# Edge masks in four 32-row products, output terms of the delta scan on VectorE, 18 chunks beside attention

## The reference

```python
# attn_a: 32 heads of 8, window 128, blocks of 128 tokens
dist = bs + r - c
valid = (dist >= 0) & (dist <= window) & (key_global >= 0)
scores = jnp.where(valid[None, None], scores, finfo.min)
out = softmax(scores) @ vw ; out @ Wo.T
# ffn: 4-bit weights plus rank-16 LoRA, 256 -> 1024 -> 256, relu
# attn_b: rms, q/k/v = silu(silu(causal_conv4(h @ W.T))), q and k l2-normed, beta = sigmoid(h @ Wbeta.T)
def step(S, inp):                      # one token, per head S is 8 x 8
    kt, qt, vt, bt = inp
    err = jnp.einsum('bhvk,bhk->bhv', S, kt) - vt
    S = S - bt[..., None, None] * err[..., None] * kt[..., None, :]
    o = jnp.einsum('bhvk,bhk->bhv', S, qt)
    return (S, o)
# then rms(o) @ Wout.T added, rms, x + (silu(gate) * up) @ Wdown.T
```

## Time and profile before

| | |
|---|---|
| median of 3 runs | 1243.53 us |
| the profiled execution | 1244.26 us, span 1242.3 us |
| busy: TensorE, VectorE, ScalarE, GpSimd | 1037.7, 917.8, 495.8, 179.0 us |
| mean granted TensorE clock | 0.905 |
| a full body (one period, ffn product L1503 of block 4 to that of block 5) | 662.1 to 797.2 us |

### The profile page before, as it was taken

The page is one execution under the profiler, slowest core; times in us unless marked ns, Lnnn a source line. Parts: engine busy times, 40 slices in busy tenths (PEclk is TensorE's granted clock), DMA queues, the critical chain, the costliest instruction groups (busy, mean ns, idle before and its releaser), DMA issues.

```text
span 1242.3 us, 23054 instructions
## 1 busy us (share of the span) xinstructions
PE 1037.7 (84%) x9098; PEld 712.3 (57%) x9112; DVE 917.8 (74%) x2425; ACT 495.8 (40%) x1027; POOL 179.0 (14%) x267
## 2 busy tenths in 40 slices
PE   3589869967998999899988999899989978966467
PEld 2245635645556665666566755666566646744445
DVE  2733277898789778987898778977898678968911
ACT  2034254326443554326432644355443634541122
POOL 2200001040004000400040000300040004010400
PEclk9579879886999899989999999989998979997768
DMA  9813014302430133012410242014400200020000
GB/s 285 153 35 76 17 43 102 61 1 72 101 50 1 35 109 79 9 35 81 89 28 10 77 100 45 1 42 103 82 7 26 82 16 1 18 77 0 5 21 9
DMA packets 94123, 67.81 MB, mean 55 GB/s; under 512 B 47744, under 2 KB 86848, under 8 KB 94016
## 3 DMA queue, kind: packets, MB, share of 16 engines
q1 hardware_dynamic: 88544, 60.75, 20.9%
q10 hardware_dynamic: 4960, 5.54, 1.6%
q0 software_dynamic: 512, 0.05, 0.1%
HBM read 45.57 MB, written 20.32 MB: 53 GB/s over the span
## 4 chain that ended last, share of the span: by engine, by line
PE 47%; DVE 28%; ACT 9%; DMA 7%; SPq 4%; issue 3%; POOL 1%; ACTq 0%; DVEq 0%; POOLq 0%
PE bank L1612 6%; PE bank L1503 5%; PE bank L1757 5%; PE bank L1560 4%; PE bank L1684 4%; PE bank L1766 4%; PE bank L1592 4%; DMA q_l<-lane_q 4%; PE bank L1709 3%; DVE state L1235 3%; DVE lane_buf L1213 3%; PE bank L1555 3%; DVE state L1227 3%; DVE u_l L1222 2%; DVE mx L1023 2%
## 5 line engine op out<-in xcount | busy, mean ns | idle before, releaser
L715 ACT ACTIVATE probs<-bank 128x512 f32<-128x512 f32 x256 | 152.1, 597 | 187.4 <-PE bank L1597 187.3
L1612 PE MATMUL bank<-probs,v_ext 128*9 128x128 f32 x2048 | 164.9, 283 | 16.5 <-ACT probs L715 6.8
L1023 DVE TENSOR_REDUCE mx<-bank 128x2 f32<-128x320 f32 x256 | 120.9, 486 | 54.3 <-PE bank L1560 50.3
L341 POOL TENSOR_TENSOR lane_buf<-state,q_l 128x128 f32<-128x128 f32 x128 | 79.9, 654 | 339.7 <-DVEq L1242 339.7
L1757 PE MATMUL bank<-feat_c,wgu 128*128 128x256 f32 (+1 forms) x384 | 96.3, 402 | 23.6 <-DVE hid_c L1284 18.0
L1612 PEld LDWEIGHTS bank<-probs,v_ext 128*9 128x9 f32 x2048 | 91.3, 93 | 39.6 <-issue 18.0
L1592 PE MATMUL bank<-q_stack,k_stack 128*128 128x128 bf16 x1024 | 106.0, 229 | 2.7 <-DMA q_stack<-m_rows 2.7
L1555 PE MATMUL bank<-edge_mask,identb 128*128 128x128 bf16 x256 | 63.0, 246 | 52.6 <-DVE mx L1023 36.6
L1757 PEld LDWEIGHTS bank<-feat_c,wgu 128*128 128x128 f32 (+1 forms) x384 | 71.8, 192 | 44.1 <-DVE hid_c L1284 21.2
L1213 DVE TENSOR_TENSOR lane_buf<-state,til 128x128 f32<-128x128 f32 x256 | 84.5, 330 | 16.9 <-POOL lane_buf L602 10.2
L1560 PE MATMUL bank<-k_stack,q_stack 128*32 128x160 bf16 x2048 | 93.0, 265 | 0.0
(11 more groups left out here) (169 smaller groups left out, 1762.5 us busy)
## 6 DMA issues: line engine op xcount, KB each, us to landing
k_pieces<-conv SPq DMA_DIRECT2D x48, 128.0 KB, 2.3
k_stack<-k_pieces SPq DMA_DIRECT2D x32, 192.0 KB
k_stack<-k_pieces SPq DMA_DIRECT2D x32, 128.0 KB
k_l<-lane_k SPq DMA_DIRECT2D x8, 512.0 KB, 3.7
q_l<-lane_q SPq DMA_DIRECT2D x8, 512.0 KB, 5.7
q_pieces<-conv SPq DMA_DIRECT2D x24, 128.0 KB, 2.1
q_stack<-q_pieces SPq DMA_DIRECT2D x32, 96.0 KB
tok<-in_x SPq DMA_DIRECT2D x8, 256.0 KB, 3.2
```

Source lines behind the costliest of these rows:

```text
L715: act.activation(probs[:, u % 2], score_bank[u % 2][:], ACT.Exp, scale=float(DK) ** -0.5).then_inc(exp_done, 1)
L1023: dve.tensor_reduce(mx[:, g, 2 * v:2 * v + 2], bank[1 + u % 2][:].rearrange("p (h k) -> p h k", h=2)[:, :, 0:SPAN], AX.X, ALU.max).then_in ...
L1612: last = pe.matmul(bank[5][row:row + VE, col:col + W], v_ext[:, b, kb, h, :], probs[:, u % 2, (hp * 2 + kb) * W:(hp * 2 + kb + 1) * W], st ...
```

## The change

1. **Edge masks.** The one full product (128 columns of the identity, output to 128 rows) becomes four, each with 32 columns of the identity and output to 32 rows.
2. **Output terms.** GpSimd's terms go. For each half VectorE now does one `step_terms` (128 x 1024 outputs) and one `state_terms` (128 x 2048). `mm_` is stored by chunk, and the terms by chunk, so that the innermost runs are 4 and 8 neighbours. For that ScalarE copies the queries into `q_t` in four parts (`queries_out`, 128 x 256 each, in attention steps 14 to 17, over `sqk`) and the states of each half into `s_t` (`states_out`, 128 x 512, over `til`). `scanned` now fires twice, after chunk 21 and after chunk 31.
3. **Order.** Slots: 3 or 4 in steps 18 to 24, 2 in steps 25 to 32, which makes 18 chunks beside the attention. `CUTS` = 18, 21, 22 and `LATE_CUTS` = 22, 24, 26, 29, 32. `first_sums` and the first half's terms come before `act_of(s, 4)`.

```diff
@@ -57,6 +57,7 @@
 TURN_AT = 20
+QUERIES_AT = 14, 15, 16, 17
 UPG = HPH // 2
@@ -162,7 +163,7 @@
         v_l = sqk[:, 1].rearrange("p (v t) -> p v t", v=VR)
-        mm_ = sb("mm_", [128, C, C, NC_])
+        mm_ = sb("mm_", [128, NC_, C, C])
         til = sb("til", [128, NC_, C, KV])
@@ -172,7 +173,10 @@
-        out_terms = lane_buf[:, 0:VR * W // 2 * (DK + C)].rearrange("p (v c i e) -> p v c i e", v=VR, i=C, e=DK + C)
+        out_terms = lane_buf[:, 0:VR * W // 2 * (DK + C)].rearrange("p (c v i e) -> p c v i e", v=VR, i=C, e=DK + C)
+        q_t = sqk[:].rearrange("p s x -> p (s x)").rearrange("p (c i k) -> p c i k", i=C, k=DK)
+        s_t = til[:].rearrange("p c i k -> p (c i k)").rearrange("p (a x) -> p a x", a=2)[
+            :, :, 0:NC_ // 2 * VR * DK].rearrange("p a (c v k) -> p a c v k", v=VR, k=DK)
         o_l = k_l[:].rearrange("p k t -> p (k t)")[:, 0:VR * W].rearrange("p (v c i) -> p v c i", v=VR, i=C)
...
@@ -332,20 +337,21 @@
-        def terms_of(engine, cs, steps=range(C)):
-            qc = q_l[:].rearrange("p k (c i) -> p i c k", i=C)
-            n_c = cs.stop - cs.start
-            for i in steps:
-                for v in range(VR):
-                    engine.tensor_tensor(out_terms[:, v, :, i, 0:DK].rearrange("p c (k e) -> p c k e", e=2),
-                                         state[:, cs, v, :, C:C + 2],
-                                         qc[:, i, cs, :].rearrange("p c (k e) -> p c k e", e=2), ALU.mult)
-                last = engine.tensor_tensor(
-                    out_terms[:, :, :, i, DK:DK + C],
-                    mm_[:, i, :, cs].rearrange("p j (o c) -> p o c j", o=1).broadcast_to([128, VR, n_c, C]),
-                    u_l[:, cs].rearrange("p c v j -> p v c j"), ALU.mult)
-            return last
+        def step_terms(engine, half):
+            cs = slice(half * NC_ // 2, (half + 1) * NC_ // 2)
+            return engine.tensor_tensor(
+                out_terms[:, :, :, :, DK:DK + C],
+                mm_[:, cs].rearrange("p c (o i) j -> p c o i j", o=1).broadcast_to([128, NC_ // 2, VR, C, C]),
+                u_l[:, cs].rearrange("p c v (o j) -> p c v o j", o=1).broadcast_to([128, NC_ // 2, VR, C, C]), ALU.mult)
+        def state_terms(engine, half):
+            cs = slice(half * NC_ // 2, (half + 1) * NC_ // 2)
+            return engine.tensor_tensor(
+                out_terms[:, :, :, :, 0:DK],
+                s_t[:, half].rearrange("p c v (o k) -> p c v o k", o=1).broadcast_to([128, NC_ // 2, VR, C, DK]),
+                q_t[:, cs].rearrange("p c (o i) k -> p c o i k", o=1).broadcast_to([128, NC_ // 2, VR, C, DK]), ALU.mult)
@@ -559,11 +565,6 @@
-            def first_terms(n):
-                pool.wait_ge(scanned, n + 1)
-                terms_of(pool, slice(0, NC_ // 2)).then_inc(terms_ready, 1)
             def ffn_bias(n):
@@ -589,7 +590,7 @@
                 for i in range(C):
-                    last = pool.tensor_copy(mm_[:, i, 0:i + 1, :], pair_l[:, at:at + i + 1, :])
+                    last = pool.tensor_copy(mm_[:, :, i, 0:i + 1].rearrange("p c j -> p j c"), pair_l[:, at:at + i + 1, :])
                     at += i + 1
...
@@ -721,6 +721,23 @@
                 act.copy(o_rows, bank[5][:]).then_inc(o_copied, 1)
+            def queries_out(n, part, front):
+                if part == 0:
+                    act.wait_ge(til_ready, n + 1)
+                    if front:
+                        act.wait_ge(turned_next, n + 3)
+                cs = slice(part * NC_ // 4, (part + 1) * NC_ // 4)
+                act.copy(q_t[:, cs].rearrange("p c i k -> p k (c i)"),
+                         q_l[:].rearrange("p k (c i) -> p k c i", i=C)[:, :, cs].rearrange("p k c i -> p k (c i)")
+                         ).then_inc(q_turned, 1)
+            def states_out(n, half):
+                act.wait_ge(scanned, n * 2 + half + 1)
+                act.copy(s_t[:, half].rearrange("p c v (k e) -> p (c v k) e", e=2),
+                         state[:, half * NC_ // 2:(half + 1) * NC_ // 2, :, :, C:C + 2].rearrange("p c v k e -> p (c v k) e")
+                         ).then_inc(s_copied, 1)
@@ -742,6 +759,8 @@
                                 piece_third(n + 1, s)
+                    if u in QUERIES_AT and after_p:
+                        queries_out(n - 1, QUERIES_AT.index(u), front)
                     if u == TURN_AT:
@@ -855,18 +874,25 @@
                 if following:
+                    if scan:
+                        states_out(t, 0)
                     norm_a(n, 1)
                 if tail:
                     nc.scalar.preload_act_table_set(SILU_SET)
                     gate_of(s, 0)
                     gate_of(s, 1)
                     gate_of(s, 2)
+                if scan and not following:
+                    for part in range(4):
+                        queries_out(t, part, False)
                 if following:
                     turn_a(n, 2)
                 for pair in range(FT // 2):
                     if following:
                         relu_a(n, 2 * pair)
                         relu_a(n, 2 * pair + 1)
+                    if following and scan and pair == IT - 4:
+                        states_out(t, 1)
                     if tail and pair < IT - 3:
...
@@ -956,9 +989,9 @@
         for step in range(BEGIN, N_UNITS + 1):
-            n_slots = 4
+            n_slots = 3 + step % 2 if step >= 18 else 4
             if step in PASS1:
-                n_slots = 3 - step % 2 if PASS1[step][0] else 2
+                n_slots = 2
             SLOT_AT.append(SLOT_AT[-1] + n_slots)
@@ -966,8 +999,8 @@
         OUT_AT = {SLOT_AT[step - BEGIN] + 1: g for g, step in enumerate((11, 19, 27))}
-        CUTS = SLOT_AT[-1] // 4, 23, 24
-        LATE_CUTS = 24, 26, 28, 30, NC_
+        CUTS = SLOT_AT[-1] // 4, 21, 22
+        LATE_CUTS = 22, 24, 26, 29, NC_
@@ -1240,22 +1273,26 @@
                         dve.nop().then_inc(scanned, 1)
+                    if c == NC_ - 1:
+                        dve.nop().then_inc(scanned, 1)
                 return other
             def reduce_terms(half):
                 cs = slice(half * NC_ // 2, (half + 1) * NC_ // 2)
-                return dve.tensor_reduce(o_l[:, :, cs], out_terms, AX.X, ALU.add)
-            def first_sums(n):
-                dve.wait_ge(terms_ready, n + 1)
-                dve.wait_ge(pairs_kept, n + 1)
+                return dve.tensor_reduce(o_l[:, :, cs].rearrange("p v c i -> p c v i"), out_terms, AX.X, ALU.add)
+            def half_steps(half, before):
+                dve.wait_ge(vstep, before)
+                step_terms(dve, half)
+            def half_states(n, half):
+                dve.wait_ge(q_turned, n * 4 + 2 + 2 * half)
+                dve.wait_ge(s_copied, n * 2 + 1 + half)
+                return mark(state_terms(dve, half))
+            def first_sums(before):
+                dve.wait_ge(vstep, before)
                 return mark(reduce_terms(0))
-            def second_terms(i, before):
-                if i == 0:
-                    dve.wait_ge(vstep, before)
-                return mark(terms_of(dve, slice(NC_ // 2, NC_), range(i, i + 1)))
...
@@ -1369,17 +1406,17 @@
                 if has_scan:
-                    step = first_sums(t)
+                    dve.wait_ge(pairs_kept, t + 1)
+                    half_steps(0, steps)
+                    step = first_sums(half_states(t, 0))
                 if tail:
                     act_of(s, 4)
                 if has_scan:
-                    step = second_terms(0, step)
-                    step = second_terms(1, step)
+                    half_steps(1, step)
                 if tail:
                     act_of(s, 5)
                 if has_scan:
-                    step = second_terms(2, step)
-                    step = second_terms(3, step)
+                    step = half_states(t, 1)
                 if following:
@@ -1552,9 +1589,11 @@
                 pb = bank[1 + u % 2][:]
-                pe.matmul(pb.rearrange("p (h e t) -> p h e t", h=2, e=2)[:, :, :, 0:SUB], identb[:],
-                          edge_mask[:].rearrange("p (o e t) -> p o e t", o=1, e=2)
-                          .broadcast_to([128, 2, 2, SUB]), start=True, stop=False, skip_group_check=True)
+                for s in range(W // SUB):
+                    rows = slice(s * SUB, (s + 1) * SUB)
+                    pe.matmul(pb[rows].rearrange("p (h e t) -> p h e t", h=2, e=2)[:, :, :, 0:SUB], identb[:, rows],
+                              edge_mask[:].rearrange("p (o e t) -> p o e t", o=1, e=2)
+                              .broadcast_to([128, 2, 2, SUB]), start=True, stop=False, skip_group_check=True)
                 for hp in range(2):
                     for s in range(W // SUB):
                         last = pe.matmul(pb[s * SUB:(s + 1) * SUB, hp * 2 * W:hp * 2 * W + SPAN],
```

(10 more changed lines are left out.)

6 lines of the change are left out of this document (2 added, 4 removed).

## The result

The changed kernel took 1237.4 us (median of 20 runs, 1232.4 to 1245.4) where the kernel before took 1244.2 (20 runs): a ratio of 0.995, interval 0.9934 to 0.9966, so 6.2 us faster where 12.4 were forecast. A second measurement of the same instructions gave 0.9922 (0.9896 to 0.9947). The direction and the range hold; the gain is half to three quarters of the forecast.

What follows compares the result with a forecast made beforehand. Neither TensorE nor VectorE alone bounds the kernel; they take turns. Gains of 35.7 less costs of 23.3 net -12.4 against the profiled 1244.26, 1231.9; the median lies 0.7 lower, so 1231 us, range 1217 to 1249.

Steps and rivals of the forecast that it cites:

- Edge masks, 0.19 a unit: Attention edge masks: four quarter products save 0.19 us a unit where TensorE sets the pace, bounds 0.09 and 0.2.
- Where this counts: Summed mask savings: steps 25 to 32 10.6, steps 14 to 17 9.6, maxima after attention 7.6, after `second_residual` 4.9, start 1.5.
- Hand-over, +0.9 a body net: Before `first_apply`: ScalarE's waiting copy of states delays `act_of(0)` to 10.2 us after the pieces from 9.24, 0.9 us a body.
- VectorE up to `second_residual`, +2.8 a body: VectorE's chain puts `second_residual` 36.1 us after the pieces, before 33.28: 2.8 a body with the hand-over, 16.8 in six bodies.
- rival 3: VectorE's new terms before `second_residual` run at the old 1.7 ns an output, not 1.04: slower, 1263 us; 8%.
- the line on two or three slots there: Attention steps 25 to 32: VectorE can follow the new 1.16 us step with two slots; the old 20 chunks had 2 or 3.
- After `second_residual`, -4.9: Eight maxima after `second_residual`: TensorE's quicker masks take about 0.7 us off, seven times, 4.9 gained.
- Last scan, -1.5: Last scan: VectorE operations no longer stretched by GpSimd's terms, about 1.5 us gained, all on the chain.
- Small things, 0.2 a body for the queries' copies: Attention step 16: `queries_out`, four copies of 0.4 us, can hold up only this step, 0.2 a body, 1.4 in all.
- Clock, +3: Longer TensorE waits, as at the gate and MLP products, may lower the clock: 3.0 us allowed, between 0 and 17.
- Rival 2: Clock falls at the gate products as TensorE's wait grows: 10 to 20 us in place of 3, 1238 to 1248; 13%.
- C: Theory formed after the first measurement, before the follow-up experiments: what is lost of the forecast gain is lost to the clock.

Runs made afterwards that it cites:

- the later copy: Changed kernel with ScalarE's copy of the first half's states moved from ahead of `norm_a` to behind the first two relus: 1225.9 us, 0.986 of the kernel before.
- the queries moved: Changed kernel with the four copies of the queries at steps 18, 27, 28, 29 in place of 14 to 17: 1237.0 us, 0.9942 of the kernel before.
- the earlier maxima: Changed kernel with the last group's maxima (unit 24 on) turned and sent at step 19, not 20: 1235.6 us, 0.9917 of the kernel before.
- both mends: Changed kernel, 18 chunks, with the first states' copy behind the first two relus and the last group's maxima sent at step 19: 1224.0 us, 0.9816 of the kernel before.

## Why the prediction was half right

- **Edge masks, 0.19 a unit: right, 0.22.** But not at all units. In steps 25 to 32 two of eight gain nothing: 1.3 us a body for 1.5. Steps 14 to 17, from exponential to exponential, took 48.9 us in bodies 0 to 5 together before, 44.8 and 46.5 in the two profiles after: 4.1 and 2.4 gained for 6.6, and 7.7 where the queries' copies are out of them. In body 1 these steps took 9.08 before and 9.21 after, where the wait ahead of the masks of step 15 grew from 1.28 to 1.73 by just what the masks before it had saved. From the last exponential to `first_residual` 1.33 to 2.45 a body for 1.1, but that is luck: with the full mask back it is 11.87 where the changed kernel has 11.42, so the masks gave 0.45 there and not 0.8, and the rest came with the other parts of the change.
- **The step that failed** is "Where this counts": it paid nearly every saved piece of TensorE's time out as time of the kernel. It left out the 16 units at the start that stand in front of a load, but it had neither the transfers of body -1 and of unit 24 in it nor VectorE's pace at the start ("SyncE's queue has nothing new" is true, and beside the point). By the run with the full mask back, all masks gave 23 us for 32.2 forecast (interval of either ratio: 4 us or less), the rest of the change cost 16.7 for 19.8, the clock's 3.0 included: the gain that is missing is missing in the masks.
- **Where it went.** At the start and in body -1 6.0 us were forecast; -1.7 and +1.2 came in the two profiles, and TensorE's waits there grew by 5.6 and 6.2, for the stacks' loads and for VectorE's maxima. Over all profiles this stretch is 190.6 and 193.0 with the full mask, 191.0 in the mean of seven with narrow masks (188.8 to 194.3) and 188.8 in five that send the maxima a step sooner (186.2 to 191.2). Up to `first_residual` in bodies 0 to 6 22.6 were forecast, 12.9 and 15.4 came; with the full mask back it is 389.5, so of 22.0 that the masks were to give there they gave 6.1 and 8.6, with the maxima sent a step sooner 17.0. At unit 24 the saving is turned into a wait for the max rows, and in body 4 into half clock. The landing, not the lead alone, decides: with step 20 kept, the kernels with the later copy and with the queries moved waited only 1.25 and 1.79 us in body 4 and gained 20.6 and 22.2 there. In all kernels with step 20, the maxima took 2.9 to 3.0 us from issue to use, and were not waited for, wherever the DMA engines were busy 23% or less meanwhile, and 4.1 us or more wherever that share was 49% or more.
- **Hand-over, +0.9 a body net: right as a landmark**, `act_of(0)` 10.0 us after the pieces for 10.2 (9.24 before), wrong as a choice. From `first_residual` on, 4.70 became 5.96. But with `norm_a` ahead of the copy it is 4.16, which I did not work out: 8 to 11 us lay there.
- **VectorE up to `second_residual`, +2.8 a body: right.** 35.8 us after the pieces for 36.1 (33.28 before). From `first_residual` on it is 3.0 more in nine of ten full bodies (28.7 to 31.7 or 31.8; once 33.0, with 6.8 us at half clock), body 0 2.5 for 2.1. `step_terms` 1.22 and `state_terms` 2.28 us against 1.2 and 2.3 forecast: rival 3 did not occur. That "the two chunks that left the attention" are what costs is shown by the run with 20 chunks; that they left steps which VectorE would not have paced is what I had wrong, in the line on two or three slots there.
- **After `second_residual`, -4.9 (4.2 of it in bodies 0 to 6): too small.** 7.6 and 7.9 came; part of it is less half clock there (44 and 51 us for 58), part is taken from the stretch ahead. With this stretch and the one up to `first_residual` together, 26.8 were forecast, 20.6 and 23.4 came, and 24.7 to 27.0 with the later copy, the queries moved, the earlier maxima or both mends: what is lost in one of the two comes back in part in the other.
- **Last scan, -1.5: right, and hidden in the changed kernel's own profiles** (+1.6 and +1.8). Nine other kernels with the same last scan take 134.2 to 136.7 us for it, 135.8 in the mean, and three with GpSimd's terms 137.1 to 137.4. In the changed kernel's two profiles the MLP product behind the last gate ran at 0.58 and 0.56 of the clock over 11 us, 0.84 before:

```profile
1133.51:1144.51 11.00, 10.50 (x24) 7.03 (x24) 6.28 (x21) 0.00 (x0) 0.00 (x0) 0.58 0.00 0
```

- **Small things, 0.2 a body for the queries' copies:** they took 0.66 us each, the bound and not the 0.4 of the sum; 0.5 a body in the steps, nothing at the end.
- **Clock, +3: about right in size.** The granted clock of the runs is 0.906 in the median (20 runs) against 0.908 (43 runs of the kernel before), 232 and 228 us at half clock. The two profiled executions had more, 239 and 246 (236 before). Rival 2 expected the fall at the gate products; in full bodies 3.4 to 6.8 us at half clock came in four of the ten of the two profiles, and cost time only where they were 6.8, since VectorE sets that stretch. C is not what took the gain, though it adds to the wait in body 4.

What stays open: the share of the clock in the 22 us that 20 chunks give, why the place of the queries' copies costs nothing at the end, and why the stretch up to the next scan grows where the one ahead shrinks. The best kernels measured are the changed one with its old 20 chunks (0.9771) and the two of that kind with the earlier maxima (0.976, 0.9765), which can't be told apart: 2.3 to 2.4% under the kernel before, where the change as made gives 0.5 to 0.8%.

## What to carry to other kernels

Time saved on an engine counts only as far as the next thing that does not move with it: follow the quicker engine to its next load, and send that load sooner by as much. When a copy that waits is put in front of short work of the same engine, price it against the order in which the short work goes first, not against the kernel before. Work that fits beside another engine's steps should leave them only if those steps are shown to wait for it.

## What the runs showed of the hardware

Four quarter products in place of one full product among narrow ones save TensorE 0.22 us a unit, of which 0.09 is product time; the other 0.13 is the passage from narrow to full and back, or the overlap with the value products, which no run here separates. A copy of 48 x 128 bf16 (12 KB) took 6.4 us from issue to use while the stack loads kept the DMA engines 65% busy. In a wait of 3.4 us the granted clock fell to its lower level, and was there for 6.8 us in all; none followed waits of 1.25, 1.48 and 1.56 us at the same product of body 4, 3.4 us of it one of 1.79. GpSimd's copies into the new `mm_`, four in each of eight scans, cost 15.8 us in all against 12.7, its writes now apart, and nobody waited for them. ScalarE's copy of the queries (256 elements, written apart) took 0.66 us, as long as that of the states with twice as many (512, read in pairs), 0.65; a plain copy of 512 takes 0.59:

```profile
L732 ACT COPY sqk<-q_l 128x256 f32<-128x256 f32 x32 | 20.4, 657 | 0.0
...
L738 ACT COPY til<-state 128x512 f32<-128x512 f32 x16 | 10.4, 649 | 34.2 <-DVEq L1275 18.4 <-DVEq L1277 15.8
```
